# Affine parts moved into evictions, TensorE's step in another order, and ones multiplied ahead of the first transposes

## The chip, the cores and the metric

The kernel runs on one core of a Trainium2 chip. The metric is the device time of one execution in microseconds. The engines are named as in the profile: PE (TensorE matmuls) with PEld (its weight loads), DVE (VectorE), ACT (ScalarE), POOL (GpSimd) and SP (SyncE, which issues the DMAs).

## The reference

2048 tokens (8 sequences of 256) of width 512 pass through two stages. In short form:

```
h = layernorm(x) @ Win.T + bin                      # 64 wide
for L in range(4):                                  # DEPTH
    y = silu(layernorm(h) * l1w + l1b)
    h = h + conv(y) * scl                           # a decaying complex recurrence along the sequence
    y = layernorm(h) * ln2_w + ln2_b
    y = silu(y @ W1.T + b1)                         # 256 wide
    h = h + y @ W2.T + b2
x = x + layernorm((layernorm(h) * lnl_w + lnl_b) @ Wout.T + bout)
x = x + layernorm(memory_read_and_gate(layernorm(x)))   # top 8 of 128 slots, softmax, gate
```

## The kernel before

The 2048 tokens are 16 tiles of 128, in 4 groups (`g`) of 4 tiles. One group in one layer is a unit `u` (16 units, `g = u % 4`, `L = u // 4`). The 64-wide state `H[g]` stays in PSUM, one bank for each group. Five programs, one for each engine, are written out by hand; an engine does its instructions in the written order, and they wait for each other by semaphores. No scheduler orders anything. The state is kept centred (the weights that feed it have their mean taken out), so that a layernorm needs only a sum of squares and a factor.

A unit passes through four steps `s` of the loop, and each step works on up to four units at once. In step `s` the pieces are, with the names and lines of the kernel before:

- On PE: `project(s-3)` adds `pick` x `B2W` (L1147, the bias b2) and the product of `HD` and `ffst` (L1153, 8 matmuls) to `H`; `turn2(s-2)` (L1125, 2 transposes), `turn1(s)` (L1094, 4 transposes), `mix_in(s-1)` (L1107), for the first steps `first_h` (L1082), and `hidden(s-2)` (L1139).
- On ACT: `square` of H for unit `s+1` (L471), `z_out(s-2)` (L485), `silu1(s)` (L476), `square(s-1)`, and two `silu2(s-2)` (L492), one for each half `a` of the 256 hidden columns.
- On DVE: `scan(s-1)` (L793), `scale(s-2)` (L776), `scale_twice(s)` (L768), `demodulate(s-1)` (L799), `sum_squares(s+1)` (L762), `modulate(s)` (L784), `sum_squares(s-1)`.
- On POOL: `norm` (L327), which raises a sum of squares to the power -0.5, once for `ss1` and once for `ss2` in each step.

`turn1(u)` needs `scale_twice(u)`, which needs `norm(u)`, `sum_squares(u)`, `square(u)`, and those need `H[g]` after `project(u-4)`, which is PE's work of step `u-1`.

Around the loop stands constant work. `setup_ffn` on PE computes W1 x ln2_b (L1037, which needs the DMA `c<-in_c`) and the centred W2 (L1042) behind step 0. `ffn_weights` on ACT scales W1 by ln2_w (L422). `setup_late` prepares the second stage from step 4 on, `wo_bias` (L725, L728) and `score_rows` (L733 to L738, six instructions) are DVE's share of it. `ffn_constants` on DVE in step 1 splits b2 into three bf16 parts. Behind the loop stand the output product (L1183), the scores (L1207) and the memory read (L1251).

Of the kernel before, what the change touches and what calls it, by code (L numbers as in the profile page):

```python
# [26 lines left out]
ALU = mybir.AluOpType  # L27
# [16 lines left out]
HW = GW // 2  # L44
VC = VOCAB // P
# [19 lines left out]
for _n, _k in (("b2", DEPTH), ("lw", 1), ("lb", 1), ("wout", VOCAB),  # L65
               ("wrt", RDIM), ("keys", NSLOT), ("wq", VOCAB)):
    C64[_n] = (_at, _at + _k)
    _at += _k
# [8 lines left out]
NFF = 2 * P + 2  # L77
# [4 lines left out]
def build(nc, x, xT, win, binb, ch, c64, w1d, w2n, b1, b2b, late, wu1, wr, wvu, boutr, srow, out):  # L82


    with ExitStack() as ctx:
# [3 lines left out]
        def sem(name):  # L89
# [16 lines left out]
        w1r = sb("w1r", [P, DEPTH * DFF + DEPTH])  # L106
        w2r = sb("w2r", [DIM, DEPTH * DFF])
# [11 lines left out]
        w1st = sb("w1st", [P, DEPTH, DFF])  # L119
# [14 lines left out]
        lbp = sb("lbp", [DIM, DIM + 1])  # L134
# [44 lines left out]
        W2B = bank[7]  # L179
# [7 lines left out]
        s_ch, s_win, s_w1, s_c64, s_w2, s_late, s_rows = (sem(n) for n in (  # L187
            "s_ch", "s_win", "s_w1", "s_c64", "s_w2", "s_late", "s_rows"))
        s_xt = [sem(f"s_xt{g}") for g in range(GROUPS)]
        s_x = [sem(f"s_x{g}") for g in range(GROUPS)]  # L190
        pool_const = sem("pool_const")
# [6 lines left out]
        b1_mm, b1_read, act_step = sem("b1_mm"), sem("b1_read"), sem("act_step")  # L198
        wo_row, sums_ready, sums_scaled = sem("wo_row"), sem("sums_ready"), sem("sums_scaled")
        cv_store, table_done, ff_done, b2_done = sem("cv_store"), sem("table_done"), sem("ff_done"), sem("b2_done")  # L200
# [3 lines left out]
        w1_store = sem("w1_store")  # L204
# [50 lines left out]
        LATE0, LATES = 4, 7  # L255
# [6 lines left out]
        def _(sp):  # L262
# [3 lines left out]
            for g in range(GROUPS):  # L266
                sp.dma_start(XT[:, g, :, :], xT[:, g]).then_inc(s_xt[g], 16)
                sp.dma_start(X[:, g * GT:(g + 1) * GT, :], x_v[g]).then_inc(s_x[g], 16)
                if g == 1:
                    sp.dma_start(w1r[:, :], w1d).then_inc(s_w1, 16)  # L270
                    sp.dma_start(w2r[:, :], w2n).then_inc(s_w2, 16)
                    sp.dma_start(b1r[:, :], b1).then_inc(s_w2, 16)
                    sp.dma_start(b2r[:, :, :], b2b).then_inc(s_w2, 16)
                if g == 3:
# [4 lines left out]
                    sp.dma_start(WOR[DIM:DIM + 1, :], boutr).then_inc(s_rows, 16)  # L279
# [10 lines left out]
        def _(pool):  # L290
# [15 lines left out]
            pool.memset(lbp[:, :], 0.0).then_inc(pool_const, 1)  # L306
# [41 lines left out]
            pool.memset(ZL[DIM:P, :, :], 0.0).then_inc(pool_zero, 1)  # L348
            pool.wait_ge(pool_zero, 1)
            pool.memset(ZL[DIM:DIM + 1, :, :], 1.0).then_inc(pool_zero, 1)  # L350
            pool.wait_ge(pool_zero, 2)
            input_rstd(0)
            for s in range(STEPS - EARLY):
                step(s)
                if s == 3:
                    pool.wait_ge(rs1, s + 2)
                    pool.wait_ge(rs2, s)
                    pool.memset(WO[DIM:P, :], 0.0).then_inc(pool_zero, 1)
                    pool.wait_ge(pool_zero, 3)
                if s == 11:  # L360

                    pool.wait_ge(sums_ready, 2)
# [21 lines left out]
        def _(act):  # L384
            act.wait_ge(pool_const, 1)
# [33 lines left out]
            def ffn_weights():  # L419
                act.wait_ge(s_w1, 16)  # L420
                for L in range(DEPTH):
                    act.activation(w1st[:, L, :], w1r[:, L * DFF:(L + 1) * DFF], ACT.Copy,  # L422
                                   scale=w1r[:, DEPTH * DFF + L:DEPTH * DFF + L + 1]).then_inc(w1_store, 1)

            def ffn_out():
                act.wait_ge(b1_mm, 1)
                act.activation(sm[:, 8:16], LB[:, 0:8], ACT.Copy).then_inc(b1_read, 1)
                act.wait_ge(w2_mm, 1)
                for L in range(DEPTH):
# [877 lines left out]
```

## Time and profile before

| | us |
|---|---|
| median of 3 runs | 260.06 (257.82 to 260.46) |
| the profiled execution, whole | 259.15 |
| its span in the profile | 257.4 |
| PE, DVE, ACT, POOL busy | 203.1, 182.4, 127.2, 93.7 |
| granted TensorE clock, mean | 0.934 of full |

The span is what the profiler saw between first and last instruction; 1.75 us of the execution lie around it. The busy times add up over stages with different limits, so none of them says what bounds a stage. An execution of this kernel differs from the next by up to 2.6 us here.

### The profile page before, as it was taken

The numbers are of one execution on the slowest core, as the hardware profiler recorded it, in microseconds if no ns is written. First come the engines' busy times: TensorE is split into PE (matmuls) and PEld (weight loads), VectorE is DVE, ScalarE is ACT, GpSimd is POOL, SyncE is SP. The second block draws the span as 40 slices with busy tenths as digits, with TensorE's granted clock in tenths as the row PEclk, the third lists the DMA queues.
The fourth block names the chain that finished last, engine by engine and source line by source line (L and its number), as shares of the span: only waits on it lengthen the run. The fifth ranks groups of instructions, "written<-read, shape, count | busy, mean of one in ns | idle before, by whom it ended". The sixth has DMA issues, their size and how long they took to land.

```text
span 257.4 us, 3466 instructions
## 1 busy us (share of the span) xinstructions
PE 203.1 (79%) x1122; PEld 148.2 (58%) x1122; DVE 182.4 (71%) x510; ACT 127.2 (49%) x314; POOL 93.7 (36%) x119
## 2 busy tenths in 40 slices
PE   2865499688888899988777866999999999679800
PEld 2855499487576778866666633655656555233300
DVE  7899855367769666777774137479777795879994
ACT  3429603745554566646555345434342327769640
POOL 2714214155142445544554123221222210018972
PEclk9997956869999999999999999999999999979975
DMA  6999900000000000000000000000000000002446
GB/s 217 425 360 423 232 7 0 1 3 0 1 3 0 0 3 0 3 1 0 0 3 0 0 0 4 0 1 0 3 0 0 0 0 1 0 3 83 163 163 244
DMA packets 5267, 15.09 MB, mean 59 GB/s; under 512 B 897, under 2 KB 1761, under 8 KB 4226
## 3 DMA queue, kind: packets, MB, share of 16 engines
q1 hardware_dynamic: 5250, 14.88, 16.0%
q8 instruction: 9, 0.15, 0.2%
q14 instruction: 8, 0.07, 0.1%
HBM read 10.68 MB, written 4.19 MB: 58 GB/s over the span
## 4 chain that ended last, share of the span: by engine, by line
PE 57%; ACT 14%; DVE 10%; DMA 9%; issue 3%; SPq 3%; POOL 2%; POOLq 0%; DVEq 0%; ACTq 0%
PE bank L1207 14%; PE bank L1153 12%; DMA c<-in_c 9%; PE bank L1139 7%; ACT HD L492 6%; PE bank L1107 5%; PE bank L1183 5%; PE bank L1094 3%; PE bank L1251 3%; PE bank L1194 2%; ACT U L553 2%; PE bank L1082 2%; PE bank L1042 1%; DVE X L1007 1%; PE bank L1037 1%
## 5 line engine op out<-in xcount | busy, mean ns | idle before, releaser
L327 POOL TENSOR_TENSOR RS<-SS,nhalf 128x4 f32<-128x4 f32 x36 | 47.5, 1321 | 75.4 <-DVE SS L762 75.4
L1153 PE MATMUL bank<-ffst,HD 128*128 128x128 f32 x256 | 34.6, 290 | 13.0 <-ACT HD L492 12.9
L1207 PE MATMUL bank<-SW_,Y 128*128 128x384 f32 x128 | 43.9, 485 | 0.0
L1153 PEld LDWEIGHTS bank<-ffst,HD 128*128 128x128 f32 x256 | 31.4, 200 | 16.1 <-ACT HD L492 16.1
L471 ACT ACTIVATE SQ<-bank 128x256 f32<-128x256 f32 x36 | 13.9, 385 | 40.9 <-PE bank L1153 31.6
L1207 PEld LDWEIGHTS bank<-SW_,Y 128*128 128x128 f32 x128 | 23.9, 190 | 17.0 <-issue 4.2
L492 ACT ACTIVATE HD<-bank,ffst 128x512 f32<-128x512 f32 x32 | 20.2, 683 | 11.4 <-PE bank L1139 11.4
L762 DVE TENSOR_REDUCE SS<-SQ 128x4 f32<-128x260 f32 x36 | 15.1, 419 | 12.1 <-ACT SQ L471 12.0
L1139 PE MATMUL bank<-Z,w1st 64*128 64x256 f32 x128 | 18.9, 416 | 2.2 <-ACT Z L485 2.1
L844 DVE SCALAR_TENSOR_TENSOR X<-bank,OR,X 128x512 f32<-128x512 f32 x16 | 11.3, 747 | 12.8 <-POOL OR L345 12.6
L784 DVE TENSOR_TENSOR U<-Y,cvst 128x514 f32<-128x514 f32 x16 | 11.1, 694 | 12.3 <-ACT Y L476 12.3
L1082 PE MATMUL bank<-wcc,XT 128*128 128x128 f32 x128 | 19.0, 321 | 0.8 <-DVE wcc L651 0.8
L793 DVE TENSOR_TENSOR_SCAN V<-cvst,U 128x514 f32<-128x514 f32 x16 | 19.5, 1220 | 0.1
L1082 PEld LDWEIGHTS bank<-wcc,XT 128*128 128x128 f32 x128 | 18.9, 238 | 1.0 <-DMA XT<-in_xT 1.0
L532 ACT ACTIVATE V<-bank 128x128 f32<-128x128 f32 x16 | 4.3, 277 | 28.4 <-PE bank L1207 28.4
L1107 PE MATMUL bank<-cvst,U 128*128 128x128 f32 x128 | 18.1, 286 | 0.0
L776 DVE TENSOR_TENSOR Z<-bank,RS 128x256 f32<-128x256 f32 x20 | 8.3, 423 | 13.6 <-POOL RS L327 13.6
L1183 PE MATMUL bank<-WO,ZL 128*128 128x512 f32 x32 | 16.2, 597 | 2.1 <-DVE X L844 2.1
L1251 PE MATMUL bank<-V,U 128*128 128x512 f32 x32 | 16.4, 643 | 0.7 <-ACT U L558 0.7
L1107 PEld LDWEIGHTS bank<-cvst,U 128*128 128x128 f32 x128 | 16.4, 200 | 0.5 <-DVE U L799 0.5
L476 ACT ACTIVATE Y<-bank,cvst 128x512 f32<-128x512 f32 x16 | 12.4, 777 | 8.3 <-PE bank L1094 8.2
L1094 PE MATMUL bank<-ident,Z 128*128 128x128 f32 x64 | 10.8, 295 | 5.8 <-DVE Z L768 5.8
(228 smaller groups left out, 381.5 us busy)
## 6 DMA issues: line engine op xcount, KB each, us to landing
XT<-in_xT SPq DMA_DIRECT2D x4, 1024.0 KB, 11.5
X<-in_x SPq DMA_DIRECT2D x4, 1024.0 KB, 13.5
out<-X SPq DMA_DIRECT2D x8, 512.0 KB, 2.8
w1r<-in_w1d SPq DMA_DIRECT2D x1, 514.0 KB, 13.1
lt<-in_late SPq DMA_DIRECT2D x1, 385.5 KB, 19.3
c<-in_c SPq DMA_DIRECT2D x1, 301.5 KB, 22.4
w2r<-in_w2n SPq DMA_DIRECT2D x1, 256.0 KB, 12.1
SW_<-in_wu SPq DMA_DIRECT2D x1, 256.0 KB
```

Source lines behind the costliest of these rows:

```text
L327: pool.tensor_tensor(RS[:, g, :], SS[:, g, :], nhalf[:, :], ALU.pow).then_inc(done, 1)
L492: act.activation(HD[:, u % 2, a, :].rearrange("p (h n) -> p h n", h=2), FB[a], ACT.Silu, bias=ffst[:, L, 2 * P + a:2 * P + a + 1]).then_in ...
L762: dve.tensor_reduce(SS[:, g, :], SQ[:, g, :, :], AX.X, ALU.add).then_inc(done, 1)
L793: dve.tensor_tensor_scan(V[:, g, :], cvst[:, L, DC0:DC0 + UC], U[:, g, :], 0.0, ALU.mult, ALU.add).then_inc(v1, 1)
L1082: last = pe.matmul(HK[g][:, j * P:(j + 1) * P], XT[:, g, c, j * P:(j + 1) * P], wcc[:, c, :], start=(j == 0 and c == 0), stop=(c == VC - 1 ...
L1094: last = pe.transpose(T1B[:, j * P:(j + 1) * P], Z[:, g, j * P:(j + 1) * P], ident[:, :])
L1107: last = pe.matmul(HK[g][:, j * P:(j + 1) * P], U[:, g, j * P:(j + 1) * P], cvst[:, L, MX0:MX0 + P], start=False, stop=True, skip_group_ch ...
L1139: last = pe.matmul(FB[a][:, h, :], w1st[h * DIM:(h + 1) * DIM, L, a * P:(a + 1) * P], Z2[h * DIM:(h + 1) * DIM, g, :], start=True, stop=True)
L1153: last = pe.matmul(HK[g][:, j * P:(j + 1) * P], HD[:, u % 2, a, at:at + P], ffst[:, L, a * P:(a + 1) * P], start=False, stop=True, skip_gr ...
L1183: pe.matmul(OB[t % 2][:, :], ZL[:, t // GT, (t % GT) * P:(t % GT + 1) * P], WO[:, :], start=True, stop=True).then_inc(o_mm, 1)
L1207: last = pe.matmul(SBK[t % 4][:, 0:SW], XNT[:, t % 4, c * P:(c + 1) * P], SW_[:, c, :], start=False, stop=(c == VC - 1))
L1251: pe.matmul(MB[t % 4][:, :], ET[:, t // 2 % 2, (t % 2) * P:(t % 2 + 1) * P], V2[:, :], start=True, stop=True).then_inc(aux_mm, 1)
```

## The change

The change has six parts, in one diff.

1. **Affine parts.** ln2_w and ln2_b are the scale and bias of `z_out`'s activation, lnl_w and lnl_b those of `last_z`. `ffn_weights`, `hidden_bias`, `wo_bias`, `lb_column` and the matmuls L1037 and L1050 go; `silu2` takes b1 as it was loaded. Wout and bout come in one DMA, and `output_sums` (ACT) adds their columns up.
2. **setup_ffn** is only the centring of W2, with a DMA of its own behind the first group of x, and stands between the first two `first_h` on PE. `ffn_out` on ACT has two evictions where there were five.
3. **PE's step** begins with `turn1(s)`, ahead of `project(s-3)`; `project` runs over `a` outside and over tiles inside, and waits for each half of `silu2` by itself.
4. **ACT's step** does `silu1(s)` ahead of `square(s+1)` and `z_out(s-2)`.
5. **DVE's step** does `scale_twice(s)` first, then `scan(s-1)`, `scale(s-2)` and `demodulate(s-1)` (from step 4 on; before that the order is `sum_squares(s)`, `scan`, `scale_twice`, `scale`). POOL writes its constants ahead of the first power.
6. **keep_busy**: 10 matmuls of ones into a part of a PSUM bank that nobody reads, ahead of `turn1(0)`, and 6 each ahead of `turn1(1)` and `turn1(2)`. They wait for nothing.

```diff
+            def keep_busy(n):
+
+                for _ in range(n):
+                    pe.matmul(T2B[:, HW:HW + P], ones[:, :], ones[:, :], start=True, stop=True)
+
             def turn1(u):
                 g = u % GROUPS
+                if u < 3:
+                    keep_busy(10 if u == 0 else 6)
                 pe.wait_ge(z1, u + 1)
...
-                pe.wait_ge(g2, 2 * u + 2)
-                for j in range(GT):
-                    at = (j % 2) * HW + j // 2 * P
-                    for a in range(2):
+                for a in range(2):
+                    pe.wait_ge(g2, 2 * u + a + 1)
+                    for j in range(GT):
+                        at = (j % 2) * HW + j // 2 * P
                         last = pe.matmul(HK[g][:, j * P:(j + 1) * P], HD[:, u % 2, a, at:at + P],
                                          ffst[:, L, a * P:(a + 1) * P], start=False, stop=True,
                                          skip_group_check=True)
...
             def step(s):
                 ffn = 0 <= s - 2 < UNITS
+                turn1(s)
                 if 0 <= s - 3 < UNITS:
                     project(s - 3)
                 if ffn:
                     turn2(s - 2)
-                turn1(s)
...
             first_h(0)
+            setup_ffn()
             first_h(1)
             for s in range(STEPS - EARLY):
                 step(s)
-                if s == 0:
-                    setup_ffn()
...
             def z_out(u):
+                L = u // GROUPS
                 act.wait_ge(t2, u + 1)
-                act.activation(Z2[:, u % GROUPS, :], T2B[:, 0:HW], ACT.Copy).then_inc(e2, 1)
+                if u == 0:
+                    act.wait_ge(s_w1, 32)
+                act.activation(Z2[:, u % GROUPS, :], T2B[:, 0:HW], ACT.Identity, scale=w1r[:, W1W + L:W1W + L + 1],
+                               bias=w1r[:, W1B + L:W1B + L + 1]).then_inc(e2, 1)
...
                 conv = 0 <= s - 1 < UNITS
-                if conv:
-                    scan(s - 1)
...
-                if 0 <= s - 2 < UNITS:
-                    scale(s - 2, rs2, z2)
+                if conv and s < GROUPS:
+                    scan(s - 1)
                 if s < UNITS:
                     scale_twice(s)
...
+                if conv and s >= GROUPS:
+                    scan(s - 1)
+                if 0 <= s - 2 < UNITS:
+                    scale(s - 2, rs2, z2)
                 if conv:
                     demodulate(s - 1)
...
                 ffn = 0 <= s - 2 < UNITS
+                if s < UNITS:
+                    silu1(s)
+                else:
+                    last_z(s)
                 if GROUPS <= s + 1 < STEPS:
                     square(s + 1, (a2, s - GROUPS + 2), sq1)
                 if ffn:
                     z_out(s - 2)
-                if s < UNITS:
-                    silu1(s)
-                else:
-                    last_z(s)
```

On PE, at the end of step 7 of the loop (L1139 is `hidden(5)`, L1065 a piece of `setup_late`) and in step 8, before:

```order
L1139 MATMUL bank<-Z,w1st 128x256 x4
L1065 MATMUL bank<-rkT,wr_s 64x128
L1147 MATMUL bank<-B2W,pick 128x4x64
L1153 MATMUL bank<-ffst,HD 128x128 x8
L1125 MATMUL bank<-ident,Z 128x128 x2
L1094 MATMUL bank<-ident,Z 128x128 x4
L1107 MATMUL bank<-cvst,U 128x128 x4
L1139 MATMUL bank<-Z,w1st 128x256 x4
```

The same stretch after; L1095 is `hidden`, L1057 `turn1`, L1104 and L1110 are `project`, L1082 `turn2`, L1070 `mix_in`:

```order
L1095 MATMUL bank<-Z,w1r 128x256 x4
L1021 MATMUL bank<-rkT,wr_s 64x128
L1057 MATMUL bank<-ident,Z 128x128 x4
L1104 MATMUL bank<-B2W,pick 128x4x64
L1110 MATMUL bank<-ffst,HD 128x128 x8
L1082 MATMUL bank<-ident,Z 128x128 x2
L1070 MATMUL bank<-cvst,U 128x128 x4
```

`turn1` now stands between `hidden` and `project`, in the place where PE waited for `silu2`.

On DVE, one loop step before (L793 `scan`, L776 `scale`, L768 `scale_twice`, L799 `demodulate`, L762 `sum_squares`, L784 `modulate`):

```order
L793 SCALAR_TENSOR_TENSOR V<-cvst,U 128x514
L776 TENSOR_TENSOR Z<-bank,RS 128x256
L768 TENSOR_TENSOR Z<-bank,RS 128x512
L799 TENSOR_TENSOR U<-V,cvst 128x512
L762 TENSOR_REDUCE SS<-SQ 128x4
L784 TENSOR_TENSOR U<-Y,cvst 128x514
L762 TENSOR_REDUCE SS<-SQ 128x4
```

And after, in the same order of names L735 `scale_twice`, L760 `scan`, L743 `scale`, L766 `demodulate`, L729 `sum_squares`, L751 `modulate`:

```order
L735 TENSOR_TENSOR Z<-bank,RS 128x512
L760 SCALAR_TENSOR_TENSOR V<-cvst,U 128x514
L743 TENSOR_TENSOR Z<-bank,RS 128x256
L766 TENSOR_TENSOR U<-V,cvst 128x512
L729 TENSOR_REDUCE SS<-SQ 128x4
L751 TENSOR_TENSOR U<-Y,cvst 128x514
L729 TENSOR_REDUCE SS<-SQ 128x4
```

`scale_twice` moved from behind the scan and the other scaling to the front of the step, right behind the last `sum_squares` of the step before.

On PE at the start, before (L1082 `first_h`, L1094 `turn1`, L1037 and L1042 `setup_ffn`, L1107 `mix_in`):

```order
L1082 MATMUL bank<-wcc,XT 128x128 x32
L1094 MATMUL bank<-ident,Z 128x128 x4
L1082 MATMUL bank<-wcc,XT 128x128 x16
L1037 MATMUL bank<-c,w1r 128x1 x8
L1042 MATMUL bank<-centre,w2r 128x64 x8
L1094 MATMUL bank<-ident,Z 128x128 x4
L1107 MATMUL bank<-cvst,U 128x128 x4
L1082 MATMUL bank<-wcc,XT 128x128 x16
```

And after (L1038 `first_h`, L1002 `setup_ffn`, L1046 `keep_busy`, L1057 `turn1`, L1070 `mix_in`):

```order
L1038 MATMUL bank<-wcc,XT 128x128 x16
L1002 MATMUL bank<-centre,w2r 128x64 x8
L1038 MATMUL bank<-wcc,XT 128x128 x16
L1046 MATMUL bank<-ones 128x128 x10
L1057 MATMUL bank<-ident,Z 128x128 x4
L1038 MATMUL bank<-wcc,XT 128x128 x16
L1046 MATMUL bank<-ones 128x128 x6
L1057 MATMUL bank<-ident,Z 128x128 x4
L1070 MATMUL bank<-cvst,U 128x128 x4
L1038 MATMUL bank<-wcc,XT 128x128 x16
```

`setup_ffn` went ahead of the second `first_h`, and the ones stand right behind a `first_h` each time, ahead of the transposes' wait.

## Rows read from the trace of the kernel before

**Rows 1.** Page of the profile, part 2: granted TensorE clock, 40 equal slices, tenths.
```profile
PEclk9997956869999999999999999999999999979975
```

**Rows 2.** Chain of waits, merged pieces: start us, us, what.
```profile
9.10 22.36 DMA c<-in_c
...
37.99 1.04 PE bank L1094 x4
...
52.40 3.79 PE bank L1153 x16
...
60.25 2.05 PE bank L1153 x16
...
146.89 2.05 PE bank L1153 x16
```

**Rows 3.** Timeline of one loop step: start us, us, engine, line, operation.
```profile
105.41 2.05 PE L1153 MATMUL bank<-ffst,HD 128*128 128x128 f32 x16 [0.29 <-ACT HD L492]
...
107.30 0.38 PE L1125 MATMUL bank<-ident,Z 128*128 128x128 f32 x2
...
107.50 0.38 ACT L471 ACTIVATE SQ<-bank 128x256 f32<-128x256 f32 x1 [1.66 <-PE bank L1153]
107.52 0.60 PE L1094 MATMUL bank<-ident,Z 128*128 128x128 f32 x4
...
107.92 0.42 DVE L762 TENSOR_REDUCE SS<-SQ 128x4 f32<-128x260 f32 x1 [0.36 <-ACT SQ L471]
107.95 1.06 PE L1107 MATMUL bank<-cvst,U 128*128 128x128 f32 x8
...
108.42 1.01 POOL L327 TENSOR_TENSOR RS<-SS,nhalf 128x4 f32<-128x4 f32 x1 [2.52 <-DVE SS L762]
...
108.94 1.14 PE L1139 MATMUL bank<-Z,w1st 64*128 64x256 f32 x8
108.96 0.69 DVE L784 TENSOR_TENSOR U<-Y,cvst 128x514 f32<-128x514 f32 x1 [0.62 <-ACT Y L476]
...
109.58 0.42 DVE L762 TENSOR_REDUCE SS<-SQ 128x4 f32<-128x260 f32 x1
109.91 1.22 DVE L793 TENSOR_TENSOR_SCAN V<-cvst,U 128x514 f32<-128x514 f32 x1
...
110.01 0.28 PE L1147 MATMUL bank<-B2W,pick 96*128 96x256 bf16 x1
110.07 1.85 POOL L327 TENSOR_TENSOR RS<-SS,nhalf 128x4 f32<-128x4 f32 x1 [0.65 <-DVE SS L762]
110.12 1.26 ACT L492 ACTIVATE HD<-bank,ffst 128x512 f32<-128x512 f32 x2 [0.69 <-PE bank L1139]
...
111.44 2.05 PE L1153 MATMUL bank<-ffst,HD 128*128 128x128 f32 x16 [1.15 <-ACT HD L492]
```

**Rows 4.** Timeline: `scale_twice`, then transposes that wait for it.
```profile
82.40 0.68 DVE L768 TENSOR_TENSOR Z<-bank,RS 128x512 f32<-128x512 f32 x1
...
83.14 0.66 PE L1094 MATMUL bank<-ident,Z 128*128 128x128 f32 x4 [0.16 <-DVE Z L768]
...
83.73 1.16 PE L1107 MATMUL bank<-cvst,U 128*128 128x128 f32 x8
```

**Rows 5.** Timeline: a VectorE product of two SBUF inputs beside a GpSimd power.
```profile
22.87 0.68 DVE L674 TENSOR_TENSOR tmpB<-cvst,CS 128x512 f32<-128x512 f32 x1
23.09 1.33 POOL L321 TENSOR_TENSOR RX<-VX,nhalf 128x4 f32<-128x4 f32 x1
```

**Rows 6.** Timeline of VectorE: first copy of `score_rows`, and the next scan.
```profile
78.25 0.35 DVE L733 CAST SWB<-SWR 96x384 bf16<-96x384 f32 x1
...
80.94 1.23 DVE L793 TENSOR_TENSOR_SCAN V<-cvst,U 128x514 f32<-128x514 f32 x1
```

**Rows 7.** Timeline: unit 1 scaled; unit 3 given its first `H`.
```profile
30.70 0.69 DVE L768 TENSOR_TENSOR Z<-bank,RS 128x512 f32<-128x512 f32 x1 [1.12 <-POOL RS L327]
...
50.30 0.87 DVE L755 SCALAR_TENSOR_TENSOR bank<-bank,RX,binc 128x64 f32<-128x64 f32 x4 [4.38 <-POOL RX L321]
```

More of the change, by code:

```diff
@@ L76, with build @@
 NCV = DC0 + UC
-NFF = 2 * P + 2
+NFF = 2 * P
 PAIRS = TILES // 2
 ROWS = 3 * 32
-def build(nc, x, xT, win, binb, ch, c64, w1d, w2n, b1, b2b, late, wu1, wr, wvu, boutr, srow, out):
+def build(nc, x, xT, win, binb, ch, c64, w1d, w2n, b1, b2b, late, wu1, wr, wvu, woutb, srow, out):
     with ExitStack() as ctx:
@@ L835, in step @@
                     sum_squares(s - 1, sq2, ss2)
-                if s == LATE0:
-                    wo_bias()
                 if s == LATE0 + 2:
@@ L1032, in setup_ffn @@
             def setup_ffn():
-                pe.wait_ge(s_w1, 16)
-                pe.wait_ge(s_c64, 16)
-                for k in range(2 * DEPTH):
-                    last = pe.matmul(LB[:, k:k + 1], w1r[0:DIM, k * P:(k + 1) * P],
-                                     c6c("b2", k // 2, k // 2 + 1), start=True, stop=True)
-                last.then_inc(b1_mm, 1)
-                pe.wait_ge(s_w2, 48)
-                for k in range(2 * DEPTH):
-                    last = pe.matmul(W2B[:, k * DIM:(k + 1) * DIM], w2r[:, k * P:(k + 1) * P], centre[0:DIM, :],
-                                     start=True, stop=True)
+                pe.wait_ge(s_w2, 16)
+                for L in range(DEPTH):
+                    for h in range(2):
+                        last = pe.matmul(W2B[h][:, L * DIM:(L + 1) * DIM], w2r[h * DIM:(h + 1) * DIM, L * P:(L + 1) * P],
+                                         centre[h * DIM:(h + 1) * DIM, :], start=True, stop=True)
                 last.then_inc(w2_mm, 1)
@@ L1047, in setup_late @@
                 if i == 0:
-                    pe.wait_ge(act_step, 1)
-                    last = pe.matmul(LB[0:DIM + 1, :], lbp[:, :], c6c("wout"), start=True, stop=True)
+                    pe.wait_ge(s_c64, 16)
+                    last = pe.matmul(LB[0:RDIM, 0:NSLOT], c6c("wrt"), c6c("keys"), start=True, stop=True)
+                if i >= 1:
+                    pe.wait_ge(late_read, i)
                 if i == 1:
-                    pe.wait_ge(wo_row, 1)
-                    last = pe.matmul(LB[0:RDIM, 0:NSLOT], c6c("wrt"), c6c("keys"), start=True, stop=True)
-                if i >= 2:
-                    pe.wait_ge(late_read, i - 1)
-                if i == 2:
                     pe.wait_ge(s_late, 48)
@@ L1063, in setup_late @@
                                          stop=(c == VC - 1))
+                if i == 2:
+                    last = pe.matmul(LB[0:BOT, 0:NSLOT], wr_s[:, :], rkT[:, :], start=True, stop=True)
                 if i == 3:
-                    last = pe.matmul(LB[0:BOT, 0:NSLOT], wr_s[:, :], rkT[:, :], start=True, stop=True)
-                if i == 4:
                     last = pe.matmul(LB[:, :], vpT[:, :], wvu_s[:, :], start=True, stop=True)
-                if i >= 5:
-                    for c in range(2 * (i - 5), 2 * (i - 5) + 2):
+                if i >= 4:
+                    for c in range(2 * (i - 4), 2 * (i - 4) + 2):
                         last = pe.matmul(LB[:, (c % 2) * 2 * NSLOT:(c % 2 + 1) * 2 * NSLOT],
@@ L1138, in hidden @@
                     for h in range(2):
-                        last = pe.matmul(FB[a][:, h, :], w1st[h * DIM:(h + 1) * DIM, L, a * P:(a + 1) * P],
+                        last = pe.matmul(FB[a][:, h, :],
+                                         w1r[h * DIM:(h + 1) * DIM, L * DFF + a * P:L * DFF + (a + 1) * P],
                                          Z2[h * DIM:(h + 1) * DIM, g, :], start=True, stop=True)
```

152 lines of the change are left out of this document (55 added, 97 removed).

## The prediction

> **What bounds the kernel now.** I read the clock and the chain of waits first. The granted clock is below full in several slices up to about 58 us, at full speed from there to about 220 us, and below it in places after that [rows 1]. In the chain, PE at the start waits for a late DMA, `c<-in_c`, which lands at 31.46 us, and only then does `setup_ffn` and, at 37.99, the transposes of unit 1; `project(0)` begins at 52.40 [rows 2]. From there to `project(15)` at 146.89 lies the loop, and behind its end, 148.94, 108.5 us of the span are output stages that the change leaves as they are (their matmuls, order and waits are the same), so I take nothing for them.
>
> The loop is read in one step [rows 3]. From `project` at 105.41 to the next at 111.44 are 6.03 us, all on one path: `project` 1.89, `turn2` 0.22, `turn1` 0.43, `mix_in` 0.99, from `hidden` to the start of `silu2` 1.18, both `silu2` 1.26, and 0.06 until PE goes on: together 6.03. PE waits in each step for the pair of `silu2`, with only the bias matmul L1147 in that gap. DVE, ACT and POOL are each waiting in between. `scale_twice` of the next unit isn't late here: its `norm` ends at 109.43, and it is merely queued behind the scan.
>
> **The loop after the change.** Call 0 the moment at which `project` has issued its last matmul (107.30 in rows 3). PE's own work behind it: `turn2` 0.22, `mix_in` 0.99, `hidden` 1.07 up to L1147, so PE is free at 2.28. `silu2`'s first half ends at 0.22 + 0.99 + 1.18 + 0.69 = 3.08 (the 0.69 is my estimate of one of the pair of 1.26, which overlap a little). If nothing else held, `turn1` (0.43) and L1147 (0.28) would run in that gap, `project` could start at 3.13 and end at 5.02: a step of 5.0, 1.0 less than now. That is the gain that the order on PE offers.
>
> But `turn1` of the next unit now stands ahead of the next `project`, and its input comes from the `project` just done. The path, from rows 3: 0.20 until `square` starts, 0.42 from there to `sum_squares`, 0.50 to `norm`, `norm` 1.01, 0.04 until DVE goes on (as from ACT's `square` to DVE's sum), `scale_twice` 0.68 and 0.06 until PE starts [rows 4]: 2.91. Then transposes that waited take 0.59 before the next group starts, where queued ones take 0.43 [rows 3, 4]. L1147 costs 0.28, and a gap of 0.10 ahead of it (hidden to L1147 takes 1.07, where `mix_in`'s like work takes 0.99; the gap is an estimate between 0 and 0.1). `project` 1.89. The sum is 2.91 + 0.59 + 0.38 + 1.89 = 5.77. `silu2` is long done, so its two separate waits give nothing.
>
> One more term comes in. `modulate` is queued right behind `sum_squares(s+1)` on DVE and its Y is ready early (ACT does `silu1` first now), so it starts about 0.33 behind the start of the sum, and the `norm` 0.50 behind it: the power runs into a product with two inputs in SBUF. Now `modulate` comes 0.54 after `norm` has started, and `norm` takes 1.01; the `norm` that starts 0.16 into the scan takes 1.85, that is, until 0.79 after the scan's end [rows 3]. A product of the same size, 0.22 before the power, makes it 1.33 [rows 5]. So `norm` goes from 1.01 to about 1.35 here (0.17 into a product of 0.69, and 0.84 behind its end), and the step to about 6.11. From both sides: 0 if POOL gets in first, 0.84 if it is held as by the scan. I take 0.34, as the nearest row is of the same shape of product. The Trainium skill bears on this (GPSIMD Engine Reference, 1. Specifications): GpSimd shares its SBUF interfaces with VectorE and contends with instructions that have two SBUF inputs. By that rule the step is 6.1, without it 5.8; the rows on 1.85 and 1.33 agree with it.
>
> So a plain step stays at about 6.1 against 6.03. PE gets its own stall back as a stall for `z1`. The cover of `scale_twice` is gone too: `score_rows` runs 78.25 to 80.94 on DVE, 2.69 us [rows 6]. After, it lies between `sum_squares(s-1)` (the second L762 in rows 3, 1.63 behind the start of `mix_in`, so issued by 0.22 + 1.63 + 0.33 = 2.18) and `scale_twice`, which can then start at 4.87 instead of 2.17 + 0.34 = 2.51. That step costs 2.3 more, about 8.3. The last three steps have no `modulate` and the single `scale` (0.42): 5.8, 5.5, 5.5.
>
> From `project(1)` to `project(15)` there are 14 steps. Before, 146.89 - 60.25 = 86.64 [rows 2], with `wo_bias` and `score_rows` in it. After, 10 x 6.11 + 8.3 + 5.8 + 2 x 5.5 = 86.2. Gain 0.4; with `norm` not held 10 x 5.77 + 8.3 + 3 x 5.5 = 82.5, gain 4.1.
>
> **The start.** PE no longer waits for `c<-in_c`; W2's own DMA (256 KB) is issued third from the front of the large ones. `turn1(1)` can start when unit 1 is scaled, at 31.4 [rows 7] instead of 37.99; the sum in front of the scan gives perhaps 0.3 more, the `norm` then being caught by the scan. What is late next: `first_h(3)` on PE starts at about 31.1 + 0.59 + 0.99 = 32.7. ACT's four squares of x for group 3 start when DVE has done `ffn_constants` and `first_h(2)`, at about 35.7, and take 2.5 to 3.4 (an estimate: 0.63 each by the pair of `silu2`, 1.26 for twice 512 columns, and up to 0.2 more for each one's sum), and POOL's add and power 1.3 (`norm` 1.01 and a small add); so unit 3 gets its H at about 41 and not at 50.30 [rows 7]. Its sum and power follow behind `silu2(0)` and under a scan (1.85), so `scale_twice(3)` ends at about 47.2, `turn1(3)` and L1147 take 1.0, and `project(0)` starts at 48.3 instead of 52.40: 4.1 earlier. At full clock it takes 1.9 where now 3.8 are shown [rows 2], and `project(1)` starts 5.9 earlier. If the clock is at half then and in `first_h(3)`, it is 3.1. I take 4.8.
>
> What hides the rest: the three ZL and WO constants on POOL lie before x has landed. If they hold DVE, it is there, where it waits for the DMAs of x anyway; uncovered, I bound them by 1.85 each, the longest POOL row shown. `z_out` and `last_z` with scale and bias may take 0.2 longer, while `mix_in` (0.99) covers `z_out`; uncovered it would be 0.2 a step, 3 in all.
>
> **keep_busy** is 22 matmuls of fp32 with 128 columns, at 0.24 each like those of `project` (1.89 / 8): 2.4 us ahead of `turn1(0)` and 1.4 twice. All of it lies in waits. It waits for nothing, so it runs right behind `first_h` and leaves the end of each wait idle: PE would be idle about 4 us ahead of 31.1. The clock fell at about 32 after such an idle stretch, and PE's `project(0)` at 3.79 against 2.05 is the price of half clock [rows 1, 2]. The skill says of this (TensorE: Matmul & The Clock Gate, What's actually happening) that the default state is throttled and activity releases the throttle; by it the ones would keep the first transposes at 2.4 GHz, and those wait for DVE anyway, so I credit them with 1 us at most, inside the 3.1 to 5.9.
>
> **Sum.** 259.15 - 4.8 - 0.4 = 253.95 for an execution like the profiled one. The median lies 0.9 above it, and PE's stall of 3.3 us in the `score_rows` step may cost one step at half clock (60.25 - 52.40 = 7.85 against 6.03: 1.8 [rows 2, 3]), which I weigh at 30%. Forecast 254.5.
>
> **Rivals.**
> (a) `norm` isn't held, or L1147 costs less: the gain is 4.8 + 4.1 to 5.5, so 249 to 251. For it: a product that starts 0.54 after a `norm` doesn't hold it. Against: rows 5. With the 5.0 step that PE alone would allow, 243; the path through `z1` excludes that.
> (b) The clock falls in the same places as now: start 3.1 earlier, step 6.2, one more step at half clock: 259.15 - 3.1 - 0.4 + 1.0 + 1.8 = 258.5, no change that can be told. For it: the idle stretches remain.
> (c) Slower: the 3.3 us that PE idles for `score_rows` drop the clock to half for several steps, at 1.82 each. For it: the clock stayed low for a slice and a half after 32 us with PE busy [rows 1]. The gain of 5 is used up after 3 such steps, and 1% is lost from 5 on: 254 + 9.1 = 263.
> (d) The folded affine parts put `z_out` on the path (3 us): 257, inside the forecast's range.
>
> **Chances.** Forecast (251.5 to 257) 0.47, (a) 0.22, (b) 0.21, (c) 0.07, others 0.03. The range 248.5 to 260.5 leaves out (c) and the ends of (a). Faster by over 1% (below 257.5) 0.70, within 1% 0.22, slower 0.08; 1% is about what a measurement of this kernel can tell from no change.
>
> **What would show it.** Right: a loop step near 6.1 in which PE waits for `scale_twice` and not for `silu2`; POOL's first `norm` of a step at about 1.35; one step of about 8.3; `turn1(1)` at about 31, `project(1)` at about 54 to 57. Wrong: a step of 5.5 or less (a link of the `z1` path is shorter than rows 3 say), a clock at half beyond 60 us, or a tail behind `project(15)` that isn't 108.5.

## The result, and the profile after

The changed kernel takes 249.95 us (median of 4 executions, 249.39 to 251.17), the kernel before 260.26 on the same chip: a ratio of 0.962, 95% interval 0.954 to 0.970. It is faster by 10.3 us, and the two profiled executions lie 8.8 us apart (259.15 and 250.35). A second set of executions gave 249.73 us and 0.954 (0.944 to 0.963). Some executions of a kernel run over 1.5% longer than its fastest one, and where that bears on a comparison it is made without them. The span of the changed kernel's profile is 248.5 us.

The granted clock, part 2 of the page of the kernel after, to be held against [rows 1]:

```profile
PEclk9999989799997999999999999999999999979965
```

Ahead of 220 us the clock is below 0.9 in three slices (8, 7, 7), each by itself, where the kernel before has 7, 9, 5, 6, 8 and 6 in a row.

The chain of waits of the kernel after at the start, merged pieces as in [rows 2]:

```profile
27.89 1.87 POOL RS L328
...
29.78 0.70 DVE Z L735
...
30.52 1.12 PE bank L1057 x4
...
49.06 2.59 PE bank L1110 x16
...
55.53 1.56 PE bank L1110 x14
```

`turn1(1)` starts at 30.52 instead of 37.99; the `norm` ahead of it is caught by a scan (1.87 us). `project(0)` starts at 49.06, `project(1)` at 55.53 instead of 60.25. No DMA stands in this part of the chain any more.

The ring of the loop in the same view, from one `norm` to the next `sum_squares`:

```profile
96.21 1.40 POOL RS L328
...
97.63 0.70 DVE Z L735
...
98.38 0.66 PE bank L1057 x4
99.03 0.11 PE bank L1104
99.14 1.80 PE bank L1110 x16
...
100.97 0.39 ACT SQ L449
...
101.38 0.44 DVE SS L729
```

The step is 5.68 us long against 6.03 [rows 3], with 0.02 to 0.07 of hand-over between two rows, and it is closed: `turn1`, `project`, `square`, `sum_squares`, `norm`, `scale_twice`, `turn1`. The timeline from one `turn1` to the next shows where PE stands and what holds `norm`:

```profile
98.38 0.66 PE L1057 MATMUL bank<-ident,Z 128*128 128x128 f32 x4 [0.95 <-DVE Z L735]
98.87 0.27 PE L1104 MATMUL bank<-B2W,pick 96*128 96x256 bf16 x1
98.98 1.95 PE L1110 MATMUL bank<-ffst,HD 128*128 128x128 f32 x16
100.97 0.39 ACT L449 ACTIVATE SQ<-bank 128x256 f32<-128x256 f32 x1 [1.12 <-PE bank L1110]
101.38 0.42 DVE L729 TENSOR_REDUCE SS<-SQ 128x4 f32<-128x260 f32 x1 [1.01 <-ACT SQ L449]
101.72 0.68 DVE L751 TENSOR_TENSOR U<-Y,cvst 128x514 f32<-128x514 f32 x1
101.89 2.36 POOL L328 TENSOR_TENSOR RS<-SS,nhalf 128x4 f32<-128x4 f32 x2 [3.31 <-DVE SS L729]
103.31 0.69 DVE L735 TENSOR_TENSOR Z<-bank,RS 128x512 f32<-128x512 f32 x1 [0.39 <-POOL RS L328]
104.05 0.66 PE L1057 MATMUL bank<-ident,Z 128*128 128x128 f32 x4 [0.95 <-DVE Z L735]
```

PE waits 0.95 us in each step, for `scale_twice` and no longer for `silu2`. GpSimd's row holds two norms (2.36 in all, the second 1.00 as in the step before), so the first takes 1.36, or 1.40 in the chain: it starts 0.17 into `modulate`.

From `project(1)` to `project(15)` (the latter in the chain at 137.65) are 82.12 us against 86.64. The step with `score_rows` takes 8.00, the one behind it 7.23 (half clock in part of it), the one with two evictions of the last constants 6.07, the last three 5.38, 5.00 and 5.01, and the others 5.67 to 5.69. From the end of `project(15)` (139.44) to the end of the span are 109.1 us, before it was 108.5; from its start it is 110.85 and 110.51, since `project` itself is shorter.

So 4.7 us of the gain are in front of `project(1)` and 4.5 in the loop.

### The profile page after: what moved, and what is told of

Same layout as the page of the kernel before. It is cut to its first block, busy times and chain, and to the rows that moved or that the text cites. A ratio compares the mean times of both kernels' runs of the same rounds, so it can differ in the third digit from the quotient of the medians.

```text
span 248.5 us, 3501 instructions
## 1 busy us (share of the span) xinstructions
PE 196.7 (79%) x1148; PEld 145.2 (58%) x1148; DVE 181.2 (73%) x507; ACT 128.3 (52%) x306; POOL 89.4 (36%) x118
## 4 chain that ended last, share of the span: by engine, by line
PE 49%; DVE 25%; POOL 10%; ACT 9%; issue 4%; POOLq 0%; DVEq 0%; ACTq 0%
PE bank L1164 15%; PE bank L1110 12%; POOL RS L328 8%; PE bank L1140 5%; PE bank L1057 4%; DVE Z L735 3%; DVE SS L729 3%; PE bank L1207 3%; PE bank L1070 2%; ACT SQ L449 2%; PE bank L1151 2%; DVE XT L966 2%; DVE X L972 2%; PE bank L1038 2%; PE bank L1095 1%
## 5 line engine op out<-in xcount | busy, mean ns | idle before, releaser
L328 POOL TENSOR_TENSOR RS<-SS,nhalf 128x4 f32<-128x4 f32 x36 | 43.1, 1209 | 72.0 <-DVE SS L729 71.8
L729 DVE TENSOR_REDUCE SS<-SQ 128x4 f32<-128x260 f32 x36 | 15.1, 423 | 26.1 <-ACT SQ L449 25.0
L1110 PE MATMUL bank<-ffst,HD 128*128 128x128 f32 x256 | 33.5, 287 | 0.0
L1110 PEld LDWEIGHTS bank<-ffst,HD 128*128 128x128 f32 x256 | 32.4, 205 | 0.3
L476 ACT ACTIVATE HD<-bank,b1r 128x512 f32<-128x512 f32 x32 | 20.3, 684 | 12.1 <-PE bank L1095 12.1
L1057 PE MATMUL bank<-ident,Z 128*128 128x128 f32 x64 | 11.5, 306 | 18.0 <-DVE Z L735 17.9
L1057 PEld LDWEIGHTS bank<-ident,Z 128*128 128x128 f32 x64 | 7.3, 151 | 23.7 <-DVE Z L735 23.7
L760 DVE TENSOR_TENSOR_SCAN V<-cvst,U 128x514 f32<-128x514 f32 x16 | 19.5, 1219 | 0.0
L1095 PE MATMUL bank<-Z,w1r 64*128 64x256 f32 x128 | 18.1, 402 | 1.6 <-ACT Z L470 1.6
L1038 PE MATMUL bank<-wcc,XT 128*128 128x128 f32 x128 | 17.3, 300 | 2.2 <-DVE wcc L633 2.2
L1038 PEld LDWEIGHTS bank<-wcc,XT 128*128 128x128 f32 x128 | 16.9, 217 | 2.5 <-issue 2.4
L1070 PE MATMUL bank<-cvst,U 128*128 128x128 f32 x128 | 17.9, 285 | 0.1
L1070 PEld LDWEIGHTS bank<-cvst,U 128*128 128x128 f32 x128 | 16.4, 201 | 0.3 <-DVE U L766 0.3
L735 DVE TENSOR_TENSOR Z<-bank,RS 128x512 f32<-128x512 f32 x16 | 11.1, 691 | 7.0 <-POOL RS L328 6.9
```

Source lines behind the costliest of these rows:

```text
L328: pool.tensor_tensor(RS[:, g, :], SS[:, g, :], nhalf[:, :], ALU.pow).then_inc(done, 1)
L476: act.activation(HD[:, u % 2, a, :].rearrange("p (h n) -> p h n", h=2), FB[a], ACT.Silu, bias=b1r[:, 2 * L + a:2 * L + a + 1]).then_inc(g2, 1)
L729: dve.tensor_reduce(SS[:, g, :], SQ[:, g, :, :], AX.X, ALU.add).then_inc(done, 1)
L760: dve.tensor_tensor_scan(V[:, g, :], cvst[:, L, DC0:DC0 + UC], U[:, g, :], 0.0, ALU.mult, ALU.add).then_inc(v1, 1)
L1038: last = pe.matmul(HK[g][:, j * P:(j + 1) * P], XT[:, g, c, j * P:(j + 1) * P], wcc[:, c, :], start=(j == 0 and c == 0), stop=(c == VC - 1 ...
L1057: last = pe.transpose(T1B[:, j * P:(j + 1) * P], Z[:, g, j * P:(j + 1) * P], ident[:, :])
```

## The experiments

All of these kernels compute the whole result. "A" in the expectations is always the same theory: the loop runs on the ring above, and the start gained because nothing waits for `c<-in_c`. The plain step is the distance of two `project` starts in the profile, at full clock where nothing else is said; the column behind it is the loop as a whole, from the start of `project(1)` to that of `project(15)`. Both are read from the timeline.

| kernel | plain step | loop, us | `project(1)` in the timeline | median, us | ratio to before |
|---|---|---|---|---|---|
| before | 6.03 | 86.64 | 60.25 | 259.8 to 261.1 in four sets | 1 |
| changed | 5.68 | 82.11 | 55.37 | 249.95 | 0.962 (0.954 to 0.970) |
| changed, again | 5.68 | 82.13 | 56.18 | 249.73 | 0.954 (0.944 to 0.963) |
| 1: no ones | 5.68 | 80.50 | 56.93 | 251.75 | 0.969 (0.965 to 0.973) |
| 2: setup_ffn late | 5.68 | 82.15 | 60.59 | 256.08 | 0.988 (0.979 to 0.997) |
| 3: modulate later | 5.47 | 80.38 | 55.73 | 248.58 | 0.957 (0.952 to 0.963) |
| 4: one wait | 5.68 | 83.29 | 56.08 | 251.41 | 0.967 (0.962 to 0.972) |
| 5: PE's order back | 6.23 | 89.48 | 55.09 | 257.81 | 0.996 (0.992 to 0.999) |
| 6: DVE's order back | 7.59 and more | 116.28 | 59.81 | 288.96 | 1.098 (1.086 to 1.110) |
| 7: before, with turn1 first | 8.02 and more | 130.16 | 66.52 | 308.39 | 1.182 (1.171 to 1.193) |
| 8: before, with the split wait | 5.68 | 82.09 | 60.47 | 256.28 | 0.978 (0.970 to 0.986) |
| 9: PE's and ACT's order back | 5.46 | 78.36 | 52.74 | 245.24 | 0.947 (0.940 to 0.955) |
| 10: 9 and modulate later | 5.48 | 79.08 | 52.76 | 247.89 | 0.958 (0.950 to 0.966) |
| 11: 9, score_rows in parts | not read | not read | not read | 243.36 | 0.928 (0.919 to 0.936) |

(The timeline puts the first product of `project` up to 0.2 us ahead of the chain's piece: 55.37 is the 55.53 above, and 82.11 the 82.12.)

**The changed kernel again**, in the same set of executions as experiments 6, 8 and 11.

> The changed kernel itself, beside the other kernels of this call, as a yardstick: 249.5 to 250.5 us, or 0.960 to 0.965 of the kernel before. If the half clock of the sixth project (7.23 us for that step in its first profile) is chance, this profile may show 5.7 there; if it follows from the idle time of TensorE in the step with score_rows, it is there again.

249.73 us and the same steps. The long step, from `project(4)` to `project(5)`, is there again: 7.34, and 7.34 or 7.35 in the profiles of experiments 2, 3 and 4. In the step with `score_rows` ahead of it PE waits 2.80 us, as these rows of the timeline of the first profile show, and `project(4)` then runs at half clock (3.47 us instead of 1.95).

```profile
70.58 0.35 DVE L700 CAST SWB<-SWR 96x384 bf16<-96x384 f32 x1
...
73.26 0.69 DVE L735 TENSOR_TENSOR Z<-bank,RS 128x512 f32<-128x512 f32 x1
...
74.01 0.70 PE L1057 MATMUL bank<-ident,Z 128*128 128x128 f32 x4 [2.80 <-DVE Z L735]
```

But the wait alone doesn't bring it. Experiment 1 has the same wait of 2.80 us, and there `project(4)` takes 1.95 and the step 5.71. So five of six profiles with this wait have the half clock behind it; what decides between the two isn't shown.

**Experiment 1, no products of ones.**

```diff
-                if u < 3:
-                    keep_busy(10 if u == 0 else 6)
```

> The changed kernel without the 22 products of ones ahead of the transposes of steps 0 to 2, and nothing else. Theory A (the time comes from the order of the work and from the waits on small inputs that went away): project(1) of the profile stays within 1 us of the 55.5 of the changed kernel, a plain step of the loop stays at 5.68 us, and the time is 250 to 252 us. Rival B (the products of ones hold TensorE's clock up, and that is what the change brings): the granted clock falls in the start as it did before, project(1) comes 2 to 4 us later, and the time is 252 to 255 us.

251.75 us and a plain step of 5.68: the time is in A's range, and below B's. `project(1)` comes 0.8 to 1.6 us later than in the two profiles of the changed kernel, at 57.1 in the chain, up to 0.6 later than A had said and short of B's 2 to 4. B's sign is there in part: the mean granted clock from 20 to 60 us is 0.83, where the changed kernel's two profiles have 0.91 and 0.87 and the kernel before 0.74. So the ones do keep some clock at the start, but they are not what the change lives on.

The 1.8 us that the median loses can't be put to one place. `project(4)` runs at full clock here (above), which takes 1.6 off the loop, so `project(15)` starts as early as in the changed kernel (137.43 against 137.48), and in the profile the loss is behind the loop: the table by stretches (us, busy time and count of PE, PEld, DVE, ACT and POOL, granted clock, DMA) has a clock of 0.96 and 0.88 there, where the changed kernel has 1.00.

```profile
136.00:150.00 14.00, 9.55 (x49) 5.33 (x46) 7.17 (x15) 6.91 (x15) 4.17 (x8) 0.96 0.00 0
150.00:160.00 10.00, 10.00 (x33) 5.71 (x32) 4.73 (x13) 4.56 (x10) 1.85 (x5) 0.88 0.01 2
```

**Experiment 2, setup_ffn where it was, waiting for what it waited for.**

```diff
             def setup_ffn():
+                pe.wait_ge(s_c64, 16)
                 pe.wait_ge(s_w2, 16)
...
             first_h(0)
-            setup_ffn()
             first_h(1)
             for s in range(STEPS - EARLY):
                 step(s)
+                if s == 0:
+                    setup_ffn()
```

> The changed kernel, but the products of setup_ffn stand behind step 0 again and wait for the input that holds the keys and Wq (the one they waited for before). The loop should be as in the changed kernel (5.68 us a step). Theory A (the start gained 4.7 us because TensorE stood at that input before): project(1) comes 4 to 6 us later, 254 to 256 us. Rival I (the input is there in time by now, or the start gained by other edits): project(1) at 55.5 to 56.5, 250 to 251 us.

The numbers are A's: `project(1)` comes 5.2 us later and the median is 6.1 us longer, with the loop unchanged. The chain of this kernel at the start:

```profile
8.31 21.56 DMA c<-in_c
...
30.01 1.12 PE bank L1003 x16
...
31.44 0.38 ACT ffst L414
31.82 0.28 ACT SQ L449
...
35.27 0.88 PE bank L1058 x4
```

The input lands at 29.88, and `turn1(1)` starts at 35.27 and not at 30.52. So with this wait back, and `setup_ffn` behind step 0, the gain of the start is gone. But it goes by another way than in the kernel before. PE is done with `setup_ffn` at 31.13 here and would be free for `turn1(1)`. What is late is ScalarE: the changed kernel has `ffn_out`, which waits for the product of W2, ahead of `square(1)`, and ScalarE idles 6.9 us for it; the kernel before has it one step later. There it is PE itself: unit 1 is scaled at 31.39 [rows 7], just when the input lands, and between that and `turn1(1)` at 37.99 stand 6.4 us of products, L1037 and L1042:

```profile
31.59 2.87 PE bank L1037 x16
34.47 3.52 PE bank L1042 x16
```

L1037 went with the affine parts. L1042's 3.52 us (the mean granted clock from 31.6 to 38 us is 0.56) are 1.12 in experiment 2, at full clock and with W2 laid out in two halves of the partitions. The experiment doesn't divide the 4.7 us between the wait, the place and these shorter products, and that its 5.2 is close to 4.7 is in part chance.

**Experiment 3, modulate behind scale_twice of the next step.**

```diff
                 if s < UNITS:
                     scale_twice(s)
...
                 if conv and s >= GROUPS:
+                    modulate(s - 1)
                     scan(s - 1)
...
-                if s < UNITS:
+                if s < GROUPS - 1:
                     modulate(s)
```

> The changed kernel, but from step 4 on VectorE does modulate behind scale_twice of the next step, just ahead of the scan that reads it, so that no product of VectorE lies beside GpSimd's norm of the first half step. Theory A (the norm on GpSimd takes 1.36 to 1.40 us because VectorE's modulate is under way, and it lies on the path): norm falls to about 1.0 us, a step from 5.68 to about 5.4 us, the time to 246 to 248 us. Rival D (the norm is held by something else, or the modulate then delays what follows it as much): step unchanged or longer, 250 us or more.

The step falls by 0.21 us, to 5.47, and the median by 1.2 to 1.4, to 248.58: A's direction, with the time 0.6 us above its range. D falls. The timeline (GpSimd's first norm of a step, and what follows on DVE):

```profile
101.15 0.42 DVE L729 TENSOR_REDUCE SS<-SQ 128x4 f32<-128x260 f32 x1 [0.28 <-ACT SQ L449]
101.65 1.01 POOL L328 TENSOR_TENSOR RS<-SS,nhalf 128x4 f32<-128x4 f32 x1 [3.18 <-DVE SS L729]
...
102.53 0.42 DVE L729 TENSOR_REDUCE SS<-SQ 128x4 f32<-128x260 f32 x1 [0.96 <-ACT SQ L449]
102.88 0.68 DVE L735 TENSOR_TENSOR Z<-bank,RS 128x512 f32<-128x512 f32 x1
```

`norm` takes 1.01 with no product of DVE beside it, and 1.36 with one. That is the whole term of the prediction. It ends at 102.66, but `scale_twice` is queued behind the other `sum_squares` of the step, which comes up at 102.53, so 0.2 of the 0.35 arrive. The rule of the Trainium skill that the prediction drew on (GPSIMD Engine Reference, 1. Specifications: GpSimd shares its SBUF interfaces with VectorE and contends with instructions of two SBUF inputs) agrees with this pair of rows.

**Experiment 4, one wait for both halves of silu2.**

```diff
+                pe.wait_ge(g2, 2 * u + 2)
                 for a in range(2):
-                    pe.wait_ge(g2, 2 * u + a + 1)
```

> The changed kernel, but project waits for both halves of the hidden units before its first large product, as before. Theory A (a plain step is set by square, sum, norm, scale and transposes, and both halves are long there when project comes up): step 5.68 us as in the changed kernel, only the steps at the end of the loop, where no transposes stand ahead, lose some 0.3 us each; 250.0 to 251.0 us. Rival C (the split wait lets project start a half earlier in each step): each of 14 steps loses 0.2 us or more, 253 us or more.

A holds for the loop and C falls: the step stays at 5.68. The last three steps take 5.49, 5.59 and 5.48 instead of 5.38, 5.00 and 5.01, 1.2 us in all. The split wait is worth those 1.2 us in the changed kernel and nothing in its plain steps. The median of 251.41 is 0.4 above A's range, which had put 0.3 us on each of the three.

**Experiment 5, PE's order back.**

```diff
-                turn1(s)
                 if 0 <= s - 3 < UNITS:
                     project(s - 3)
                 if ffn:
                     turn2(s - 2)
+                turn1(s)
```

> The changed kernel, but TensorE does turn1 behind project and turn2, as before. Theory A (ScalarE's silu1 now stands ahead of square and z_out and waits for turn1; with turn1 behind project and turn2, square waits for silu1 and comes late): the step grows from 5.68 to about 6.2 us, the time to 256 to 259 us. Rival F (TensorE's order does not matter, since it idles some 0.95 us in each step): 250 us, step 5.7.

A holds, F falls. Nearly the whole gain is gone though the start keeps its share (`project(1)` at 55.09), since the step is longer than in the kernel before. The chain of a step:

```profile
115.73 0.45 PE bank L1057 x4
...
116.21 0.78 ACT Y L454
116.99 0.27 ACT SQ L449
117.26 0.47 ACT Z L470
...
117.77 1.16 PE bank L1095 x8
```

ScalarE does `silu1` first, which waits for `turn1`, and `square` and `z_out` stand queued behind it, and behind those `hidden`. ScalarE's new order needs PE's new order.

**Experiment 6, DVE's order back.** `scan` stands at the head of the step and `scale` ahead of `scale_twice` again.

> The changed kernel, but VectorE's step has the old order (scan first, scale ahead of scale_twice). Theory A (turn1 ahead of project only bears a scale_twice that comes first on VectorE): with the scan and scale in front of it a step takes 7.6 to 8.2 us and the time is 270 to 280 us. Rival J (VectorE has enough idle time for either order): 250 to 252 us.

Slower than the kernel before by 28 us. A had the mechanism, with a price 9 us too low. The chain of a step at full clock:

```profile
123.82 1.09 POOL RS L328
...
125.18 1.62 POOL RS L328
...
126.82 0.42 DVE Z L743
127.25 0.61 DVE Z L735
```

`scale_twice` (L735) stands behind `scale` (L743), and `scale` waits for the second `norm` of the step, which runs beside the scan. PE waits 2.86 us for it in such a step, where the changed kernel has 0.95. The step takes 7.59 us, as A had it, but nine of the fifteen take 8.4 to 9.9. In eight of these `project` runs at half clock for all or part of its time (3.15 us instead of 1.80 in the step ahead of these rows), and the ninth is the step with `score_rows`. So the idle time that the order makes is paid a second time by the clock, and that second part is what the expectation lacked. The run moves the scan and `scale` together; which of them costs more isn't shown.

**Experiment 7, the kernel before with turn1 first on PE.**

> The kernel before, with one thing of the change: TensorE does turn1 ahead of project and turn2. Theory A (the order on TensorE and the orders on VectorE and ScalarE belong together: the scale_twice that turn1 waits for comes late in the kernel before, behind scale and with square behind silu of the step): project then waits for it in every step, a step takes 8 us or so instead of 6.2, and the time is 280 to 295 us. Rival E (turn1 first is by itself what shortens the loop): a step of 5.7 to 5.9 us and 254 to 257 us.

The direction is A's, and so is the shortest plain step, 8.02 us; the size was missed for the same reason. `project` is at half clock for all or part of its time in 12 of the 15 steps, which take up to 11.84 us, and the time is 308 us (its profiled execution, 309.8, is the longest of the four). So PE's order alone costs 48 us in the kernel before, and E falls.

**Experiment 8, the kernel before with the split wait.** The loop over `a` outside, each half with a wait of its own, as in the change's diff.

> The kernel before, with one thing of the change: project's products of the first half of the hidden units are issued first, on a wait for that half alone. Theory A (in the kernel before TensorE stands in each step at the second silu2, so the split wait is worth up to one silu2 less its overlap, 0.57 us; it found no use in the changed kernel because turn1 stands ahead of it): a step of 5.6 to 5.8 us instead of 6.03, the time 254 to 257 us. Rival K (it gives nothing here either, and the shorter step of the run with both orders back is VectorE's new order): a step of 6.0 us, 259 to 261 us.

A holds, K falls: 5.68 us a step from `project(9)` on, and 4.8 us off the median, by splitting one wait. Ahead of that the steps take 5.49 to 5.99 and twice over 7, as in the kernel before (7.36 and 7.18, there 7.47 and 7.54). From `project(1)` to `project(15)` are 82.09 us, as many as in the changed kernel. In the timeline PE's stall goes from 1.15 [rows 3] to 0.57, and the next thing to be late is `mix_in`, which waits for `demodulate`:

```profile
115.34 2.05 PE L1153 MATMUL bank<-ffst,HD 128*128 128x128 f32 x16 [0.57 <-ACT HD L492]
...
116.34 0.42 DVE L776 TENSOR_TENSOR Z<-bank,RS 128x256 f32<-128x256 f32 x1 [0.84 <-POOL RS L327]
116.68 0.68 DVE L768 TENSOR_TENSOR Z<-bank,RS 128x512 f32<-128x512 f32 x1
117.28 0.68 DVE L799 TENSOR_TENSOR U<-V,cvst 128x512 f32<-128x512 f32 x1
...
118.02 1.16 PE L1107 MATMUL bank<-cvst,U 128*128 128x128 f32 x8
```

**Experiment 9, PE's and ACT's order back, all else as changed.** PE as in experiment 5 (the ones stand at the head of steps 0 to 2), ScalarE with `square` and `z_out` ahead of `silu1`.

> The changed kernel, but TensorE does turn1 behind project and turn2, and ScalarE does square and z_out ahead of silu1, both as before; VectorE's order stays the new one. The products of ones stand at the head of steps 0 to 2. Theory A (a path runs from project over square, sum, norm and scale_twice to turn1 and the next project; with turn1 off the way of project it is no longer closed through TensorE in one step): step 5.3 to 5.5 us, time 245 to 248 us. Rival G (the pair of orders of TensorE and ScalarE is where the change wins in the loop): the step goes back to 6.0 to 6.2 us and the time is 254 to 258 us.

A holds again, and G falls: 245.24 us, and the step is 5.46. Chain of a step:

```profile
100.99 0.22 PE bank L1080 x2
101.21 0.44 PE bank L1055 x4
101.65 0.89 PE bank L1068 x8
102.54 1.09 PE bank L1093 x8
...
103.65 0.70 ACT HD L476
...
104.39 2.05 PE bank L1108 x16
```

Now PE's own work and one half of `silu2` are the ring: 0.22 + 0.44 + 0.89 + 1.09 + 0.70 + 2.05 + 0.06 for the hand-overs = 5.45. `mix_in` takes 0.89 and not the 1.10 of experiment 8's chain, because DVE's new order has `demodulate` ready: it ends at 100.79 in the timeline, ahead of `mix_in` at 101.48, where in experiment 8 `mix_in` waits for it. This is 0.22 a step better than the change with all its orders, and 2.6 us better in front of `project(1)`: `project(0)` no longer stands behind `turn1(3)` and starts at 43.26.

**Experiment 10, experiment 9 with the later modulate of experiment 3.**

> Both orders back as in the run before it, and modulate behind scale_twice from step 4 on. Theory A: with the orders back the norm is no longer what sets the step, so freeing it gives nothing, and modulate now stands ahead of work that the second half step waits for: step 5.5 to 5.8 us, 248 to 251 us, that is more than with the orders back alone. Rival H (the two gains add): 243 to 245 us.

H falls: the step is 5.48, with no gain from a free `norm`, since `norm` isn't on the ring here. It is 0.02 short of A's 5.5 to 5.8. The `score_rows` step is 0.54 longer (8.48 against 7.94), and from `project(1)` to `project(15)` are 79.08 us against 78.36, so the later `modulate` costs 0.7 us in the loop. The total is not settled. Three executions of 247.9 to 248.1 make the median of 247.89; the other two, 243.94 and 247.06, lie on either side of experiment 9's four (244.54 to 246.08). The profiled one, 243.94, is 2.0 below experiment 9's (245.90) because of its output stage, 110.3 us from `project(15)` on against 113.0: its granted clock from 136 to 150 us is 1.00, and experiment 9's 0.88.

**Experiment 11, experiment 9 with score_rows in four parts**, one in each of steps 6 to 9, ahead of `sum_squares(s+1)`.

> The run with both orders back, and score_rows cut into four parts, one in each of steps 6 to 9, each ahead of the sum of squares for the next unit. Theory A (the whole of score_rows in one step makes scale_twice late by some 2.5 us there, where VectorE idles in every step): the step of 7.9 us falls to about 5.5 to 6.0, others stay within 0.2 of 5.46, time 242 to 244 us. Rival L (the parts hold the sum of squares and norm in four steps instead, 0.3 to 0.7 us each): 245 us, no gain.

243.36 us (the three executions at the usual clock 242.90 to 243.70), 0.928 of the kernel before and the fastest kernel here. The total is as A has it and against L, and that is all that is shown: the step that should have become shorter couldn't be read. The profiled execution took 347.91 us, with a granted clock of 0.50 to 0.56 from 13 us to its end; `project` takes 3.28 us in it.

```profile
PEclk9755555555555555555555555555555555555555
```

## Why the prediction was right, and where it was off

The direction, faster, was right, and so was the mechanism: the start gains by what went ahead of `turn1(1)`, and PE's stall in the loop turns into a stall for `scale_twice`. The size was not. The forecast of 254.5 was 4.5 us too long, the gain nearly twice what it said, and the result lies outside the forecast's own 251.5 to 257, where rival (a) was put, 249 to 251. That is partly luck for (a): it put the whole excess on `norm` or L1147. L1147's share is 1.7 us (0.17 in ten steps), and the rest came from links that (a) doesn't name.

- **The start** was right in its size, and in its cause as far as shown. `project(1)` was to gain 4.8 and gained 4.72; experiment 2 shows that the gain hangs on `setup_ffn` not standing behind step 0 with the wait for `c<-in_c`, though by another path than in the kernel before. `turn1(1)` was put at 31.4 and came at 30.52, `project(0)` at 48.3 and came at 49.06. In the full-or-half question it landed between the two: `project(0)` took 2.59 in the chain, not 1.9 or 3.8.
- **The ring through scale_twice** was right. The path from `square` to `turn1` was 3.05 us in the sum (0.42 + 0.50 + 1.35 + 0.04 + 0.68 + 0.06) and is 3.08 (100.97 to 104.05). That `modulate` holds `norm` to 1.35 was right (1.36), and experiment 3 shows it by taking it away. PE waits for `scale_twice` and `silu2` is long done, as said (experiment 4).
- **What failed is the other half of the ring**: "transposes that waited take 0.59", "L1147 costs 0.28, and a gap of 0.10", "`project` 1.89", and 0.20 until `square` starts: 3.06 us. It is 2.59 (98.38 to 100.97). From `turn1` to the first product of `project` are 0.60 and not 0.97: the bias product L1104 starts 0.49 behind `turn1`, and the next product 0.11 behind it. The prediction took the 0.28 that stands beside the instruction for its cost. That is the time from its start to its end; queued among others it costs 0.11, the distance to the next start. Of the 0.37 that are missing here, 0.17 are this, 0.10 the gap, which isn't there, and 0.10 the transposes (0.49 for 0.59). From that product to `square` are 1.99 instead of 2.09, so `project` is 0.1 shorter than where it had stood waiting for its first input.
- These 0.44 a plain step are 3.5 us in eight steps. The last three steps were 1.4 shorter than said (5.38, 5.00 and 5.01 for 5.8, 5.5 and 5.5), `score_rows`'s 0.3 (8.00 for 8.3), and the other way the half clock behind it cost 1.1 against the sum's 6.11 (7.23 from `project(4)` to `project(5)`), which the prediction had weighed at 30% and left out of the 253.95. Together 4.1: the loop gained 4.5 where 0.4 was said. With 0.1 less gained at the start, 0.3 more from `project(15)` on and 0.1 more around the span (1.85), it adds up: 253.95 - 4.1 + 0.5 = 250.35, the profiled execution.
- **Rival (a)** was right in its second condition (L1147 costs less) and wrong in its first (`norm` is held). **Rival (b)**, no change by the clock, and **(c)**, several steps at half clock, didn't come: it was one. But (c)'s mechanism exists: in experiments 6 and 7, which are 28 and 48 us slower than the kernel before, half clock in `project` is a part of it. **Rival (d)**: `z_out` takes 0.56 instead of 0.38, the 0.2 that was said, and isn't on the ring of a plain step.
- **The ones** were credited with 1 us at most. Experiment 1 has 0.8 to 1.6 of it in front of `project(1)` and 1.8 to 2.0 in the medians; where the clock falls behind the loop moved with it, and how much of the difference is due to that stays open.
- **The tail** was said to stay at 108.5 and read 109.1. Nothing was tried on it. From the timeline's `project(15)` to the end of the span, the two profiles of the changed kernel have 111.1 and 109.8, the kernel before 110.5, so it is within the spread.

What the prediction didn't see is that the change's orders for PE and ScalarE are not needed. It had found the 1.15 us of PE's stall for the pair of `silu2`, and asked only what `turn1` would do in that gap. The split wait, which it wrote off ("its two separate waits give nothing"), gives nothing only behind `turn1`: in the kernel before it takes the step from 6.03 to 5.68 by itself, just what all the orders of the change reach together. With DVE's new order, and the rest of the change but the two orders, the step is 5.46. DVE's order without the split wait wasn't run.

## What to carry to other kernels

The orders of several engines form one ring here and can't be judged one by one: of the three that were changed, PE's alone cost 48 us in the kernel before, taking DVE's out cost 39 us and taking PE's out 8, and the best kernel has DVE's alone. Before an order is turned round to fill a stall, try the smallest cut in the wait that makes it; here a wait split in two gave as much in the loop as the reordering. And in a queue of products take an instruction's cost from start to start, since the duration beside it (0.28 for 0.11) counts the way to its end too.

## What the runs showed of the hardware that was not expected

- A stall can be paid a second time by the clock. In experiment 6 PE waits 2.86 us in a plain step; the order makes the step 7.59 us instead of 5.68, and where its `project` runs at half clock (3.15 us instead of 1.80) it is 9.2, another 1.6. That happens in eight of the fifteen steps. The 0.95 us that PE waits in each step of the changed kernel never do it: its granted clock is 1.00 from 78 to 215 us.
- In experiment 11 one execution of four had a granted clock of 0.50 to 0.56 from 13 us on and took 347.91 us instead of 243.
- A half clock early in the output stage comes and goes between kernels that do the same work there. In experiments 1, 5, 7, 8 and 9 the granted clock falls 6 to 12 us behind the start of `project(15)`, and from that start to the end of the span are 111.4 to 113.0 us. In the other eight profiles (that of experiment 11 aside) it doesn't fall there, and they have 109.8 to 111.1. What decides it isn't shown.
